# Attention and ternary FFN on one core: projection results in the score banks, the last drain of the down result at head 14, row maxima at other heads

## What is computed

```python
x = x + _layernorm(_L0_attn_ref(_layernorm(x), w_attn, b_attn, w_proj, b_proj))   # eps 1e-5
x = x + _layernorm(_L0_ffn_ref(x, w_fc, w_proj))
# attention: q, k rotated by tables that depend on the head, causal softmax(q k^T) * E**-0.5, times v,
#            heads side by side, @ w_proj + b_proj
# ffn:       bitlinear(gelu(bitlinear(x, w_fc)), w_proj)
# bitlinear(x, w): layer norm of x (eps 1e-6), product with w ternarised to {-1, 0, 1} * mean|w|
```

## Time and profile before

| | us |
|---|---|
| median of 3 runs | 1349.74 (1348.42 to 1349.87) |
| the profiled execution | 1347.23 |
| its span, first to last instruction | 1345.4 |
| mean granted clock of TensorE | 0.955 of full |
| step 0 and what is before it | 0 to about 239 |
| steps 1 to 6 | about 150 each |
| step 7 and step 8 | about 1138 to 1345 |

### The profile page before, as it was taken

The page is one execution under the profiler, slowest core; times in us unless marked ns, Lnnn a source line. Parts: engine busy times, 40 slices in busy tenths (PEclk is TensorE's granted clock), DMA queues, the critical chain, the costliest instruction groups (busy, mean ns, idle before and its releaser), DMA issues.

```text
span 1345.4 us, 24978 instructions
## 1 busy us (share of the span) xinstructions
PE 1199.9 (89%) x9364; PEld 649.4 (48%) x9364; DVE 1020.4 (76%) x2931; ACT 780.3 (58%) x1446; POOL 594.2 (44%) x636
## 2 busy tenths in 40 slices
PE   4755889999989998999999998999999998988796
PEld 2322554455545554455545554455545554554343
DVE  7588797877887797878887787868887787776532
ACT  3334864666556755666556754666466755575480
POOL 6131431691049512781149412881159312971252
PEclk9865989999999999999999999999999999999799
DMA  5441121002310113002300213002300221001000
GB/s 203 132 151 65 40 64 56 1 1 66 86 40 2 44 45 102 1 10 68 85 30 2 56 41 94 1 16 68 98 11 3 56 71 33 2 8 49 8 1 32
DMA packets 49825, 65.37 MB, mean 49 GB/s; under 512 B 8581, under 2 KB 33189, under 8 KB 49192
## 3 DMA queue, kind: packets, MB, share of 16 engines
q1 hardware_dynamic: 49704, 63.77, 16.1%
HBM read 29.89 MB, written 8.39 MB: 28 GB/s over the span
## 4 chain that ended last, share of the span: by engine, by line
PE 53%; DVE 30%; ACT 9%; POOL 3%; issue 3%; SPq 1%; DMA 1%; POOLq 0%; DVEq 0%; ACTq 0%
PE gen L489 21%; PE down L532 16%; DVE score L1097 8%; PE pv L586 4%; PE score L558 4%; DVE hT L958 4%; DVE probs L958 2%; PE score L564 2%; DVE acc_add L1074 2%; POOL rstd L1431 1%; DVE qkn L1189 1%; DVE mx L1097 1%; PE gen L549 1%; DVE bn L1126 1%; ACT qkn L752 1%
## 5 line engine op out<-in xcount | busy, mean ns | idle before, releaser
L1431 POOL TENSOR_TENSOR rstd<-veps,mhalf 128x1 f32<-128x1 f32 (+1 forms) x104 | 68.3, 657 | 486.5 <-DVE veps L1174 374.4
L808 ACT ACTIVATE probs<-score 128x512 f16<-128x512 f32 (+1 forms) x384 | 201.8, 526 | 127.8 <-PE score L558 127.8
L958 DVE TENSOR_TENSOR probs<-score,probs 128x512 f16<-128x512 f32 (+1 forms) x384 | 213.2, 595 | 69.6 <-ACT score L810 69.2
L489 PE MATMUL gen<-x2T,t1T 128*128 128x512 f16 x1024 | 242.1, 381 | 5.9 <-DVE hT L958 3.4
L532 PE MATMUL down<-t2T,hT 128*128 128x512 f16 x1024 | 233.0, 380 | 3.5 <-DVE xn L1159 3.5
L810 ACT ACTIVATE score<-score 128x512 f32<-128x512 f32 (+1 forms) x384 | 204.7, 533 | 0.0
L489 PE MATMUL gen<-xT,wa 128*128 128x512 f16 x768 | 180.0, 386 | 12.0 <-DVE wa L978 8.3
L958 DVE TENSOR_TENSOR hT<-gen,hT 128x512 f16<-128x512 f32 x160 | 108.6, 685 | 73.2 <-ACT gen L771 31.6
L1097 DVE CUSTOM_DVE_ANT_0 score<-score,mask_rows 128x512 f32<-128x512 f32 (+1 forms) x344 | 157.8, 520 | 0.0
L532 PEld LDWEIGHTS down<-t2T,hT 128*128 128x128 f16 x1024 | 96.5, 98 | 110.4 <-DVE xn L1159 4.7
L489 PEld LDWEIGHTS gen<-x2T,t1T 128*128 128x128 f16 x1024 | 96.2, 98 | 111.0 <-DVE hT L958 5.3
(11 more groups left out here) (131 smaller groups left out, 1830.5 us busy)
## 6 DMA issues: line engine op xcount, KB each, us to landing
qk<-qkn SPq DMA_DIRECT2D x384, 64.0 KB, 2.0
xo<-x SPq DMA_DIRECT2D x8, 1024.0 KB, 5.5
hT<-x SPq DMA_DIRECT2D x8, 1024.0 KB, 6.2
out<-xn SPq DMA_DIRECT2D x32, 256.0 KB, 2.2
hT<-w_fc SPq DMA_DIRECT2D x4, 1024.0 KB, 6.1
hT<-w_down SPq DMA_DIRECT2D x4, 1024.0 KB, 5.0
hT<-w_attn SPq DMA_DIRECT2D x4, 512.0 KB, 10.0
hT<-w_attn SPq DMA_DIRECT2D x1, 1024.0 KB, 8.7
```

The source lines that it names most:

```text
L489: mm = nc.tensor.matmul(bank[:, :], a, b, start=(start and n == 0), stop=(stop and n == len(pairs) - 1))
L808: nc.scalar.activation(probs[:, h % 2, HI, 512 * i:512 * i + n], score[i][:, 0:n], ACT.Exp, scale=1.0 / S_UP)
L958: return V.tensor_tensor(out, whole, hi, ALU.subtract)
```

## The change

1. `project(tb)` writes the score banks 0, 1, 2 and `pv` instead of `gen`; VectorE takes the moments straight from there, without waiting for a copy; ScalarE then applies scale and shift from PSUM in one operation (`normalise_y`), and `first_sum` is a plain addition. `copy_y` and `residual` are gone (8 ScalarE operations a step become 4).
2. `final(3)` stands at head 14 on VectorE, its moments at the start of the end part.
3. Maximum passes beside the heads: heads 5, 6, 9, 10, 13, 14 instead of 8 to 13. The late pass of the end part is gone; the up part has ten passes instead of nine (one more at block 10), the shift comes at block 14 instead of 15, and step -1 has six passes instead of seven.

```diff
-FIRST_MAX = {8: 0, 11: 1, 12: 2}
+FIRST_MAX = {8: 0, 11: 1}
...
-STEP_MAX = {8: 0, 9: 1, 10: 2, 11: 3, 12: 4, 13: 5}
-LATE_MAX = len(STEP_MAX)
-EARLY = LATE_MAX + 1
-MAX_AT = {0: 7, 2: 8, 3: 9, 5: 10, 7: 11, 8: 12, 9: 13, 11: 14, 12: 15}
-SHIFT_AT = 15
+STEP_MAX = {5: 0, 6: 1, 9: 2, 10: 3, 13: 4, 14: 5}
+EARLY = len(STEP_MAX)
+MAX_AT = {0: 6, 2: 7, 3: 8, 5: 9, 7: 10, 8: 11, 9: 12, 10: 13, 11: 14, 12: 15}
+SHIFT_AT = 14
...
+        y_banks = (*score, pv)
...
-                    bank = claim("proj", tb)
+                    if tb < 3:
+                        pe.wait_ge(s_drained, s0 + S["scores", HEADS - 1] + tb + 1)
+                    else:
+                        pe.wait_ge(pv_drained, HEADS * (j + 1))
+                    bank = y_banks[tb]
...
-                    if nxt:
-                        max_pass(LATE_MAX, 1)
                     o_turn(0)
...
-                    nc.scalar.activation(y_sb[:, tb % 2, :], bank[:, :], ACT.Copy).then_inc(y_copied, 1)
...
-                    nc.scalar.activation(xres[:, tb, :], xres[:, tb, :], ACT.Identity, bias=shift[:, LP, tb:tb + 1]
-                                         ).then_inc(xb_ready, 1)
+                    nc.scalar.activation(y_sb[:, tb % 2, :], y_banks[tb][:, :], ACT.Identity,
+                                         bias=shift[:, LP, tb:tb + 1], scale=rstd[:, LP, tb:tb + 1]
+                                         ).then_inc(y_ready, 1)
...
-                    dve.wait_ge(y_copied, n + 1)
-                    V.bn_stats(bn[:, LP, tb, :], bank_of("proj", tb)[:, :]).then_inc(g_drained, 1)
+                    dve.wait_ge(y_full, n + 1)
+                    V.bn_stats(bn[:, LP, tb, :], y_banks[tb][:, :]).then_inc(bn_done[LP], 1)
...
-                    V.scalar_tensor_tensor(out=x1[:, tb, :], in0=y_sb[:, tb % 2, :], scalar=rstd[:, LP, tb:tb + 1],
-                                           in1=xres[:, tb, :], op0=ALU.mult, op1=ALU.add).then_inc(x1_ready, 1)
+                    V.tensor_tensor(x1[:, tb, :], y_sb[:, tb % 2, :], xres[:, tb, :], ALU.add).then_inc(x1_ready, 1)
...
+                        if prev and h == HEADS - 2:
+                            final(3)
...
                     if nxt:
                         v_low(0)
+                    if prev:
+                        final_moments(3)
+                        final_terms(3)
                     o_low(0)
                     o_low(1)
-                    if nxt:
-                        maxima(LATE_MAX, 1)
-                    if prev:
-                        final(3)
-                        final_moments(3)
-                        final_terms(3)
                     y_moments(0)
```

More of the change, by code:

```diff
@@ L99, in general_plan @@
     if here:
-        for name, n in (("v", 0), ("oT", 0), ("oT", 1), ("proj", 0), ("oT", 2), ("proj", 1), ("oT", 3),
-                        ("proj", 2), ("proj", 3), ("v", 1), ("x2T", 0), ("v", 2), ("x2T", 1), ("v", 3),
+        for name, n in (("v", 0), ("oT", 0), ("oT", 1), ("oT", 2), ("oT", 3), ("v", 1), ("x2T", 0), ("v", 2), ("x2T", 1), ("v", 3),
                         ("x2T", 2), ("x2T", 3)):
@@ L120, in score_plan @@
             uses.append(("scores", h + 1))
-    if nxt:
-        uses += [("next max", h) for h in ([LATE_MAX] if here else range(EARLY))]
+    if nxt and not here:
+        uses += [("next max", h) for h in range(EARLY)]
     return {use: 3 * k for k, use in enumerate(uses)}
@@ L143, in general_bank @@
     return (at + k) % 3
-assert N_USUAL % 3 == 0 and len(FIRST_MAX) + PAIRS_BEFORE == EARLY
+assert len(FIRST_MAX) + PAIRS_BEFORE == EARLY
 def need(eng, semaphore, count):
@@ L283, in build @@
         gelu_done = sem("gelu_done")
-        oT_hi, y_copied, xb_ready, xn2_ready, x2T_hi, fin_ready = (
-            sem(n) for n in ("oT_hi", "y_copied", "xb_ready", "xn2_ready", "x2T_hi", "fin_ready"))
+        oT_hi, y_full, y_ready, xn2_ready, x2T_hi, fin_ready = (
+            sem(n) for n in ("oT_hi", "y_full", "y_ready", "xn2_ready", "x2T_hi", "fin_ready"))
         m_neg, m_hi, o_sums, o_recip, o_ready, x1_ready = (
@@ L634, in project @@
                     products(bank, [(oT[:, tb % 2, LO, c, :], wp[:, HI, c, :]) for c in range(EC)], start=False
-                             ).then_inc(g_full, 1)
+                             ).then_inc(y_full, 1)
                 def x2_turn(tb):
@@ L819, in o_turned, with normalise_y @@
                     high(oT[:, tb % 2, HI, :, :], blocks(filled("oT", tb))).then_inc(oT_hi, 1)
-                def copy_y(tb):
-                    bank = filled("proj", tb)
+                def normalise_y(tb):
+                    act.wait_ge(ln_ready[LP], TB * j + tb + 1)
                     need(act, x1_ready, TB * j + tb - 1)
-                    nc.scalar.activation(y_sb[:, tb % 2, :], bank[:, :], ACT.Copy).then_inc(y_copied, 1)
[L826 to L830, removed]
-                    nc.scalar.activation(xres[:, tb, :], xres[:, tb, :], ACT.Identity, bias=shift[:, LP, tb:tb + 1]
-                                         ).then_inc(xb_ready, 1)
+                    nc.scalar.activation(y_sb[:, tb % 2, :], y_banks[tb][:, :], ACT.Identity,
+                                         bias=shift[:, LP, tb:tb + 1], scale=rstd[:, LP, tb:tb + 1]
+                                         ).then_inc(y_ready, 1)
                 def normalise2(tb):
@@ L921, in iteration @@
                     o_turned(1)
-                    copy_y(0)
-                    o_turned(2)
                     if prev:
                         final(3)
-                    copy_y(1)
-                    residual(0)
+                    o_turned(2)
+                    normalise_y(0)
                     o_turned(3)
[L929 to L932, removed]
+                    normalise_y(1)
                     normalise2(0)
+                    normalise_y(2)
+                    normalise2(1)
+                    normalise_y(3)
                     if nxt:
                         values(1)
-                    residual(3)
-                    normalise2(1)
                     x2_turned(0)
@@ L1225, in y_moments @@
                     n = TB * j + tb
-                    dve.wait_ge(y_copied, n + 1)
-                    V.bn_stats(bn[:, LP, tb, :], bank_of("proj", tb)[:, :]).then_inc(g_drained, 1)
-                    dve.wait_ge(g_drained, g0 + G["proj", tb] + 1)
+                    dve.wait_ge(y_full, n + 1)
+                    V.bn_stats(bn[:, LP, tb, :], y_banks[tb][:, :]).then_inc(bn_done[LP], 1)
+                    dve.wait_ge(bn_done[LP], n + 1)
                     moments(LP, tb)
@@ L1235, in first_sum @@
                     n = TB * j + tb
-                    dve.wait_ge(xb_ready, n + 1)
-                    V.scalar_tensor_tensor(out=x1[:, tb, :], in0=y_sb[:, tb % 2, :], scalar=rstd[:, LP, tb:tb + 1],
-                                           in1=xres[:, tb, :], op0=ALU.mult, op1=ALU.add).then_inc(x1_ready, 1)
+                    if tb == 0:
+                        dve.wait_ge(xres_in, 16 * (j + 1))
+                    dve.wait_ge(y_ready, n + 1)
+                    V.tensor_tensor(x1[:, tb, :], y_sb[:, tb % 2, :], xres[:, tb, :], ALU.add).then_inc(x1_ready, 1)
                     dve.wait_ge(x1_ready, n + 1)
```

## The result

The change is slower: 1357.64 us median (1349.91 to 1363.37, 17 runs) against 1348.53 (1346.04 to 1349.87, 17 runs), ratio 1.0066, 95% interval 1.0051 to 1.0081. That is 9.1 us more; no change was forecast, and the prediction's own range ended at 1356. The profiled execution took 1356.18, its span 1354.4, mean granted clock 0.948. The runs of the change spread over 13.5 us, those of before over 3.8.

What follows compares the result with a forecast made beforehand. TensorE, busy 89% of the span, was taken to set the time. Terms -18.2 - 2.5 + 8.4 + 3.5 - 4.2 gave -13.0, clock +11.9, sum -1.1: 1348.6 us, no measurable change; range 1336 to 1362, own case 1343 to 1356.

Steps and rivals of the forecast that it cites:

- 3 x 0.54: Heads 8, 11 and 12: pass waits gone; with 0.47 for the product's wait at head 12, -2.1 us a step.
- End part: From first o_turn to next up: 3.0 us less in each of steps 1 to 6, -18.2; step 0 -0.5, step 7 -2.0.
- Heads, the named waits: New waits at head 5, scores(7), head 7's product (1.7 us) and head 14; with waits gone, +1.4 a step, +8.4 in six.
- The copies at head 5: Pass at head 5 waits for the copies of heads 0 to 3, landing at 460.6 against TensorE's 460.10: +0.5 us.
- Up part and first scores: Up part: one more pass and moved waits, +3.5 us in seven steps; waits before the first scores go, -4.2.
- The second six places: Around weigh(15) in six steps: waits of 0.4 + 0.5 + 1.2 us within 6 us, where the clock might fall.
- the 1.02 of step 7: Wait of 1.02 us, with smaller ones, before a fall to half clock in step 7; taken as model for new waits.
- Seven of twelve: Clock, two places in each of six steps: seven of twelve bring a spell at half clock, 1.7 us each, +11.9.
- My sentence on the Trainium skill: The skill's HAM oscillation section warns only of longer gaps and would leave the clock full, sum -13.0; prediction followed the trace.
- The clock holds: Rival, chance 0.26: waits as worked out, but clock stays full or falls once or twice; 1336.7 us, with two spells 1340.
- Every place falls: Rival, chance 0.14: clock falls at all twelve places, some for the double spell; 1357 us, up to 1367.
- The end part doesn't shorten: Rival, chance 0.08: VectorE already bounds the end part, so -18.2 becomes -6; with seven spells 1361 us.

Runs made afterwards that it cites:

- experiment 1: Changed kernel with the drains final(1) and final(2) one head earlier on VectorE (heads 7 and 11 instead of 8 and 12): 1345.28 us, 0.9999 of before.
- experiment 5: Kernel before with only the heads table of maximum passes changed (heads 5, 6, 9, 10, 13, 14): 1372.11 us, 1.0173 of before.
- experiment 9: Changed kernel, passes at heads 6, 8, 9, 10, 13, 14, maxima ahead of hidden_variance at head 6, final(1) at head 8, final(2) at 11: 1321.38 us, 0.9807.
- experiment 10: Changed kernel, passes at heads 6, 8, 9, 10, 12, 13, drains at 8 and 12, maxima ahead of hidden_variance at head 6: 1320.35 us, 0.9798 of before.
- experiment 6: Kernel before with the late pass moved to the up part, shift at block 14, six passes in step -1, old heads table: 1337.7 us, 0.9921.
- experiment 7: Kernel before with the late pass moved to the up part and final(3) at head 14, old projections and heads table: 1334.48 us, 0.99 of before.
- experiment 4: Changed kernel with only the table of maximum passes beside the heads put back (heads 8 to 13): 1330.57 us, 0.9891 of before.
- experiment 2: Changed kernel with the maxima put ahead of hidden_variance and final_terms(0) on VectorE at head 6: 1341.19 us, 0.9971 of before.
- experiment 3: Changed kernel with drains final(1), final(2) at heads 7 and 11 and the maxima ahead of hidden_variance at head 6: 1333.12 us, 0.9906 of before.
- experiment 8: Changed kernel, first two passes at heads 6 and 8, drains at heads 7 and 11, maxima ahead of hidden_variance at head 6: 1334.93 us, 0.9895 of before.
- experiment 11: The change itself, unaltered, run once more against the kernel before: 1358.5 us, 1.0081 of before.

## Why the prediction was wrong

**The terms, in us.** Measured is by the starts in the profiles of before and of the change. Each of the five more spells of steps 1 to 8 is taken as 1.7 us and stands in the row of the clock; steps -1 and 0 keep theirs.

| term | predicted | measured |
|---|---|---|
| end parts of steps 0 to 7 | -20.7 | -22.1 |
| heads of steps 1 to 6 | +8.4 | +20.9, of which 10.2 `down` |
| up parts, first scores, step 7's heads | -0.7 | 0.0 |
| steps -1 and 0 before the end part | 0 | +1.3, of which 1.7 clock |
| step 8 | 0 | +0.3 |
| clock | +11.9 | +8.5 |
| sum | -1.1 | +8.9 |

**The step that failed** is the one that put the passes taken away at "3 x 0.54" of pure gain: "*Gone:* the pass waits at 8, 11 and 12". Those waits and passes were also time in which VectorE drained `down`. I asked what is late next after the waits that the change adds, and not after those that it removes. Without a pass at heads 8 and 12, the product's low part and `final` come too late for the `down` pieces of heads 9 and 13, 0.85 us in twelve places. With this term the forecast is 1348.6 + 10.2 = 1358.8, 1.2 above the median. That it comes so near is in part luck: the clock was taken 3.4 too high and the rest of the heads, among others, 2.3 too low. Experiments 1, 5, 9 and 10 show the missed term from all sides: the drain moved, the table moved, the cover put back, and put back with nothing else changed.

**End part: right.** 3.29 us a step in steps 1 to 6 for 3.0 forecast, the last transpose 22.75 after its `o_turn` for 23.0. Step 7 is the exception: for 2.0 it gained 0.9 by the granted clock itself, 1.7 if its further spell is taken off whole. The prediction walked the three edits together; by experiments 6, 7 and 4 more than half of it is the late pass that left VectorE, and a third the new banks.

**Heads, the named waits: right in kind.** 1.64 us before the product of head 7 (1.7 forecast), by experiment 2 wholly VectorE's order. The copies at head 5 cost 0.41 us in step 2 (0.5 forecast) but 1.0 to 1.5 in steps 1, 5 and 6; scores(7) wait 0.27; `weigh(15)` and `o_turn` as said. Apart from `down` the six head parts cost 10.7 for 8.4.

**Up part and first scores: right.** Experiment 6 has them alone: head and up parts of its steps 1 to 6 sum to 1.1 us less than before; the terms of the prediction for these steps say 0.8.

**Clock: right in kind, 11.9 for 8.5, and partly in other places.** Spells of 1.7 us lost come at head 7: after the 24 waits of 1.64 to 1.81 us in the four profiles that have them (the change, its repetition, 1 and 5) 2, 5, 4 and 1 falls, twelve in all, so one in two. At the same place of the other profiles without such a wait there is none in steps 1 to 6. The second six places, around `weigh(15)` and `o_turn`, gave one spell in 24, and none in the 24 of experiments 2, 3, 8 and 9: waits of 0.3 to 1.3 us there are not like the 1.02 of step 7 that I likened them to. Nor was there a spell at head 5, where the pass waited 1.4 to 1.64 us for the copies in ten places of the change and of experiments 1, 2, 3, 5 and 11. Seven of twelve should have read three of six, and about 5. The other 3.4 of the profile are spells of steps 7 and 8. My sentence on the Trainium skill stands: TensorE: Matmul & The Clock Gate, HAM oscillation, as a rule about gaps would have left the clock full. These falls come with waits of 1.6 to 1.9 us, shorter than the gaps of that rule, and vanish when these waits do (experiments 2, 9). The section behind it on the same page of the Trainium skill, A second HAM failure mode, tells of a kernel whose clock fell and rose with frequent short idle times between groups of matmuls. This trace agrees so far as falls come with idle times shorter than that rule's; here each follows a single wait of 1.64 to 1.87 us, or of 1.34 in the one case at `o_turn`.

**The rivals.** "The clock holds" is out by experiment 11 and the spread. "Every place falls" gives the right time, 1357, for a wrong reason: one spell in two at half the places, and 10 us of a wait that it didn't have. "The end part doesn't shorten" is out by 24.20.

**Open.** Step 8 has a spell at half clock behind its 1.64 us wait for `xn` in all nine profiles with the projections in the new banks, and none in the four without, though step 8 has no projection and the wait is the same 1.63 to 1.64. It is 1.7 us. The traces show one difference, the moment of the wait: it ends 47.8 to 51.1 us after the start of the last spell of step 7 in the nine, 52.3 to 52.5 after it in the four. In the same way, the falls at head 7 do not keep to the wait: they begin from 0.9 us before its end to 0.7 after it. And step 3 has none in any of the four profiles, steps 4 and 5 have one in three of them. So of two waits of 1.64 us the moment may decide which is followed by a fall. No run moved a wait and nothing else, so this is not shown.

## What to carry to other kernels

A stall that a change removes is also time in which other engines catch up. Before counting it as gain, list what the engines behind it finish in it, and look at the next use of each buffer that they free; here that was one row, the `down` piece after head 8. When several edits come as one, time the table of positions apart from the restructuring: a ratio of 1.0066 was made of 0.989 and 1.017. And put a drain that another engine waits for ahead of short work that waits itself; that one exchange at head 6 was worth 13 us, and a better table with it a kernel 2% faster than before.

## What the runs showed of the hardware

The full clock falls to half with single waits of 1.64 to 1.87 us on a TensorE that is else busy nine tenths of the time, in about half of the cases at heads 7 and 8 (14 of 30), in none of ten of 1.4 to 1.64 at head 5, and in other steps from profile to profile, for 1.7 or 3.4 us of lost time. The fall is not tied to the start or the end of the wait, and its moment may count as well as its length. So such a stall costs more than its length here: over the 24 at head 7 the clock adds 1.0 us on average (14 x 1.7 / 24, the double spells counted twice), and taking the six away gave 2.1 us each (experiment 2). And a spread of the runs that widens from 4 to 13 us, with lost clock from 62 to 79 us, is a sign of it.
